# Token mixing beside a gated MLP: values and receptance projected in seven block products per projection

## What is computed

```python
x_prev = pad(x[:, :-1, :])
xk = x * time_mix_k + x_prev * (1.0 - time_mix_k)     # xv and xr alike
k = einsum('btd,ed->bte', xk, W_k)
v = einsum('btd,ed->bte', xv, W_v)
r = sigmoid(einsum('btd,ed->bte', xr, W_r))
wkv = _wkv_scan(k, v, time_decay, time_first)         # running maximum, sums weighted by exponentials
y = r * wkv
attn = einsum('btd,ed->bte', y, W_o)
...
h = silu(lin(x, w1_w, w1_s)) * lin(x, w2_w, w2_s)      # 256 -> 1024
h = gelu(lin(h, h1_w, h1_s))                           # 1024 -> 1024
h = gelu(lin(h, h2_w, h2_s))                           # 1024 -> 1024
out = lin(h, w3_w, w3_s)                               # 1024 -> 256
```

## Time and profile before

| | |
|---|---|
| median of 3 runs | 1473.9 us (1470.48 to 1475.95) |
| the profiled execution: time, span | 1469.84 us, 1468.1 us |
| TensorE busy | 1459.3 us, 99% |
| VectorE busy | 1136.9 us, 77% |
| ScalarE busy | 997.9 us, 68% |
| GpSimd busy | 99.6 us, 7% |
| granted TensorE clock | full in every slice (2.4 GHz) |
| DMA | 300.02 MB, mean 204 GB/s |

### The profile page before, as it was taken

How to read it: one execution, slowest core, us unless ns; L and a number is a source line. 1 busy time by engine, 2 the same in 40 slices (tenths; PEclk the granted TensorE clock), 3 DMA queues, 4 the chain that set the end, 5 groups by cost and what they waited for, 6 DMA issues and landing times.

```text
span 1468.1 us, 28022 instructions
## 1 busy us (share of the span) xinstructions
PE 1459.3 (99%) x10236; PEld 1314.6 (90%) x10236; DVE 1136.9 (77%) x1600; ACT 997.9 (68%) x1525; POOL 99.6 (7%) x128
## 2 busy tenths in 40 slices
PE   8999999999999999999999999999999999999999
PEld 7989898998989989898898989989899898998998
DVE  6786878778797786977868788687877869778655
ACT  7995665767657576675856757676576765757655
POOL 1112000010100101001010010100001010010100
PEclk9999999999999999999999999999999999999999
DMA  9988574755737467375674746657475674746654
GB/s 345 386 296 282 171 246 120 239 170 194 251 113 258 142 201 250 123 255 145 202 225 149 247 132 219 195 173 252 121 245 152 206 245 120 262 136 203 186 184 133
DMA packets 105374, 300.02 MB, mean 204 GB/s; under 512 B 10496, under 2 KB 41856, under 8 KB 103552
## 3 DMA queue, kind: packets, MB, share of 16 engines
q1 hardware_dynamic: 97184, 291.75, 58.4%
q0 software_dynamic: 8160, 7.87, 4.3%
HBM read 265.44 MB, written 33.09 MB: 203 GB/s over the span
## 4 chain that ended last, share of the span: by engine, by line
PE 97%; ACT 1%; DVE 1%; issue 0%; DMA 0%; POOL 0%; DVEq 0%; SPq 0%; ACTq 0%; POOLq 0%
PE acc L713 27%; PE acc L715 27%; PE att L606 11%; PE acc L687 7%; PE acc L688 7%; PE acc L739 4%; PE acc L741 4%; PE att L645 4%; PE acc L844 2%; PE acc L842 2%; PE att L585 1%; PE att L688 1%; PE att L687 1%; PE acc L813 1%; ACT early L1246 0%
## 5 line engine op out<-in xcount | busy, mean ns | idle before, releaser
L713 PE MATMUL acc<-op_hi,ring 128*128 128x256 f32 x3360 | 810.3, 286 | 0.5 <-issue 0.5
L715 PE MATMUL acc<-op_lo,ring 128*128 128x256 f32 x3360 | 788.5, 279 | 0.0
L713 PEld LDWEIGHTS acc<-op_hi,ring 128*128 128x128 f32 x3360 | 631.0, 188 | 18.6 <-issue 17.6
L715 PEld LDWEIGHTS acc<-op_lo,ring 128*128 128x128 f32 x3360 | 632.2, 188 | 11.1 <-issue 10.0
L1716 DVE TENSOR_TENSOR op_lo<-blocks,op_hi 128x1024 fp32r<-128x1024 f32 (+2 forms) x271 | 339.4, 1268 | 66.5 <-ACT op_hi L1111 60.2
L1111 ACT ACTIVATE op_hi<-blocks 128x1024 fp32r<-128x1024 f32 (+2 forms) x263 | 284.5, 1093 | 111.9 <-DVE blocks L1711 68.6
L687 PE MATMUL acc<-x_hi,w_rnd 128*128 128x512 f32 x420 | 167.1, 398 | 0.3 <-DVE blocks L1702 0.3
L688 PE MATMUL acc<-x_lo,w_rnd 128*128 128x512 f32 x420 | 166.1, 396 | 0.0
L1151 ACT ACTIVATE blocks<-acc,vec 128x256 f32<-128x256 f32 x268 | 104.9, 476 | 68.2 <-PE acc L715 60.9
L1151 ACT ACTIVATE blocks<-parts,vec 128x256 f32<-128x256 f32 x240 | 101.1, 498 | 64.1 <-DVE parts L1774 61.5
L1107 ACT ACTIVATE fresh<-acc,vec 128x512 f32<-128x512 f32 x105 | 72.1, 686 | 74.8 <-PE acc L688 74.8
(11 more groups left out here) (216 smaller groups left out, 1904.7 us busy)
## 6 DMA issues: line engine op xcount, KB each, us to landing
ring<-scratch SPq DMA_DIRECT2D x426, 512.0 KB, 4.2
scratch<-stage SPq DMA_DIRECT2D x11, 1024.0 KB, 12.2
stage<-in_w_ffn SPq DMA_DIRECT2D x10, 1024.0 KB, 10.7
x_in<-in_x SPq DMA_DIRECT2D x32, 256.0 KB, 4.6
out<-x_next SPq DMA_DIRECT2D x30, 256.0 KB, 4.4
out<-mix_v POOLq DMA_DIRECT2D x30, 256.0 KB, 4.2
mix_r<-in_x_T SPq DMA_DIRECT2D x14, 512.0 KB, 5.7
norm<-norm_rows SPq DMA_DIRECT2D x14, 512.0 KB, 4.4
```

What stands on the lines that cost most here:

```text
L713: pe.matmul(out, act(w), act(op_hi[:, k, c, :]), start=(begins and c == 0 and m % 2 == 0), stop=False, skip_group_check=True)
L715: mm = pe.matmul(out, act(w), act(op_lo[:, k, c, :]), start=False, stop=(c == QC - 1), skip_group_check=True)
```

## The change

In the loop, for values (w = 0) and receptance (w = 1), the 256x256 weight and the 256x512 input are each taken as 2x2 blocks (an input block is a chunk of channels of one sequence). The input differences T2, T3, T4 are formed beforehand: for the values by VectorE (`quad_inputs`, into `r_sb`), for the receptance by GpSimd (`receptance_inputs`, into `mix_v`). The weight sums S1 to S4 are formed once by GpSimd (`sum_mixing`), with the values' weights scaled by 0.25 first, so that their copies need no scale. Seven products of 256 columns take the place of four of 512. They stand in four parts of 2, 2, 2 and 1 products, with `att` as four quadrants: Q11, QT3, Q21, Q22. Between the parts ScalarE copies quadrants (`again`: Q11 to Q21, then Q21 to Q22 and QT3 to SBUF), VectorE adds QT3 to Q21 and Q22 (`quad_sums`), and ScalarE takes out Q11 and Q22 (`copy_quads`). The keys, tiles 0 and 1 and the output projection are as before.

```diff
@@ -144,7 +144,7 @@
-    DVE_EXTRA = 4
+    DVE_EXTRA = 2
@@ -196,6 +196,7 @@
+w_sums = overlay("w_sums", [P, 2, 4, P], F32)
@@ -285,9 +286,21 @@
+quad = [att[:, SEG * k:SEG * (k + 1)] for k in range(4)]
+Q11, QT3, Q21, Q22 = quad
+QUADS = ((mix_v, r_sb, v_sb), (mix_r, mix_v, r_sb))
+def quarters(t):
+    return t[:].rearrange("p c (n t) -> p (c n) t", n=n_seq)
...
+def by_half(ap):
+    return ap.rearrange("p (n t) -> p n t", n=n_seq)
@@ -343,7 +356,7 @@
-               Chain(ctx, nc, "dve_chain", 38), Chain(ctx, nc, "pool_chain", 2), ahead=1, seqs_ahead=0, like=FIRST[0])
+               Chain(ctx, nc, "dve_chain", 40), Chain(ctx, nc, "pool_chain", 4), ahead=1, seqs_ahead=0, like=FIRST[0])
@@ -369,6 +382,9 @@
+dve_quad, act_again, pe_part = (tally(n, k, 1, ahead=-2) for n, k in (("dve_quad", 3), ("act_again", 4), ("pe_part", 4)))
+pool_T = tally("pool_T", 1, 1, ahead=-2)
+mix_sums = ctx.enter_context(nc.semaphore("mix_sums"))
@@ -607,6 +623,36 @@
+    def product(w, bank, weights, moving, start=False, stop=False):
+        return pe.matmul(bank, weights, moving, start=start, stop=stop, skip_group_check=True)
+    def project_part(t, w, part):
+        src, sums = quarters(QUADS[w][0]), quarters(QUADS[w][1])
+        T_1, T_3, T_2, T_4 = (sums[:, k, :] for k in range(4))
+        a11, a12, a22 = (wm[:, 1 + w, c, e * P:(e + 1) * P] for e, c in ((0, 0), (0, 1), (1, 1)))
+        S_1, S_2, S_3, S_4 = (w_sums[:, w, k, :] for k in range(4))
+        if part == 0:
+            pe.wait_ge(mix_sums, 5)
+            if w == 0:
+                pe.wait_ge(dve_quad.sem, dve_quad.at(t, 1))
+            else:
+                pe.wait_ge(pool_T.sem, pool_T.at(t))
+            pe.wait_ge(WHOLE.act_kvr.sem, WHOLE.act_kvr.at(t, 2 * w + 2))
+            product(w, Q11, a11, src[:, 0, :], start=True)
+            pe_part.add(product(w, QT3, S_3, T_3, stop=True))
+        elif part == 1:
+            pe.wait_ge(act_again.sem, act_again.at(t, 2 * w + 1))
+            product(w, Q11, a12, src[:, 2, :], stop=True)
+            pe_part.add(product(w, Q21, S_2, T_2))
+        elif part == 2:
+            pe.wait_ge(WHOLE.act_kvr.sem, WHOLE.act_kvr.at(t, 2 * w + 3))
+            product(w, Q21, a22, T_4, stop=True)
+            WHOLE.pe_kvr.add(product(w, Q22, S_1, T_1))
+        else:
+            pe.wait_ge(dve_quad.sem, dve_quad.at(t, w + 2))
+            WHOLE.pe_kvr.add(product(w, Q22, S_4, src[:, 3, :], stop=True))
@@ -903,17 +949,25 @@
             step(i, 0, 0)
             step(i, 0, 1)
             pe.wait_ge(dve_prod.sem, dve_prod.at(i, 3))
-            project(WHOLE, i + 1, [0, 1, 2])
+            project(WHOLE, i + 1, [0, 1])
             step(i, 0, 2, [0])
+            project_part(i + 1, 0, 0)
             step(i, 0, 2, [1])
-            project(WHOLE, i + 1, [3])
-            step(i, 0, 3)
-            step(i, 0, 4)
+            project_part(i + 1, 0, 1)
+            step(i, 0, 3, [0])
+            project_part(i + 1, 0, 2)
+            step(i, 0, 3, [1])
+            step(i, 0, 4, [0])
+            project_part(i + 1, 0, 3)
+            step(i, 0, 4, [1])
             step(i, 0, 5)
-            project(WHOLE, i + 1, [4])
-            step(i, 0, 6)
+            project_part(i + 1, 1, 0)
+            step(i, 0, 6, [0])
+            project_part(i + 1, 1, 1)
+            step(i, 0, 6, [1])
+            project_part(i + 1, 1, 2)
             step(i, 1, 0, [0])
-            project(WHOLE, i + 1, [5])
+            project_part(i + 1, 1, 3)
             step(i, 1, 0, [1])
             step(i, 1, 1)
             step(i, 1, 2)
@@ -1047,6 +1101,20 @@
+    def again(t, w, k):
+        if k == 0:
+            act.wait_ge(pe_part.sem, pe_part.at(t, 2 * w + 1))
+            act_again.add(act.activation(Q21, Q11, ACT.Copy))
+        else:
+            act.wait_ge(pe_part.sem, pe_part.at(t, 2 * w + 2))
+            WHOLE.act_kvr.add(act.activation(Q22, Q21, ACT.Copy))
+            act_again.add(act.activation(QUADS[w][2][:, 0, 0:SEG], QT3, ACT.Copy))
+    def copy_quads(t, w):
+        act.wait_ge(WHOLE.pe_kvr.sem, WHOLE.pe_kvr.at(t, 2 * w + 4))
+        WHOLE.act_kvr.add(act.activation(by_half(QUADS[w][2][:, 0, :]), att[:].rearrange("p (k t) -> p k t", t=SEG)[:, 0::3, :], ACT.Copy))
@@ -1066,6 +1134,8 @@
         act.wait_ge(s.act_kvr.sem, s.act_kvr.at(t))
+        if not isinstance(t, int):
+            act.wait_ge(dve_quad.sem, dve_quad.at(t, 3))
         s.act_exp.add(act.activation(r_sb[:, :, s.cols], r_sb[:, :, s.cols], ACT.Tanh, scale=0.5))
@@ -1381,26 +1451,28 @@
         copy_kvr(WHOLE, i + 1, [0])
         p1(i, 0)
         copy_kvr(WHOLE, i + 1, [1])
-        copy_kvr(WHOLE, i + 1, [2])
+        again(i + 1, 0, 0)
         g11(i, 0)
+        again(i + 1, 0, 1)
         hiB11(i)
         p5(i, 0)
-        copy_kvr(WHOLE, i + 1, [3])
         hi6(i)
         u2(i, 0)
+        copy_quads(i + 1, 0)
         exp_new(WHOLE, i + 1)
         exp_old(WHOLE, i + 1)
         share(WHOLE, i + 1)
+        again(i + 1, 1, 0)
         g12(i, 0)
         g22(i, 0)
+        again(i + 1, 1, 1)
         hiB22(i)
         hiT1(i)
-        copy_kvr(WHOLE, i + 1, [4])
         g21(i, 0)
+        copy_quads(i + 1, 1)
         hiT23(i)
         p1(i, 1)
         hiB21(i)
-        copy_kvr(WHOLE, i + 1, [5])
         receptance(WHOLE, i + 1)
         p5(i, 1)
         seed_x(WHOLE, i + 1)
@@ -1545,6 +1617,24 @@
+    def quad_inputs(t):
+        b, T = quarters(QUADS[0][0]), quarters(QUADS[0][1])
+        dve.wait_ge(WHOLE.dve_mix.sem, WHOLE.dve_mix.at(t, 2 * DC))
+        link(WHOLE, dve.tensor_tensor(T[:, 0:2, :], b[:, 1::2, :], b[:, 0:2, :], ALU.subtract))
+        settle(WHOLE, t)
+        link(WHOLE, dve.tensor_tensor(T[:, 2, :], b[:, 3, :], T[:, 0, :], ALU.subtract))
+        settle(WHOLE, t)
+        dve_quad.add(dve.tensor_tensor(T[:, 3, :], b[:, 2, :], T[:, 2, :], ALU.subtract))
+    def quad_sums(t, w):
+        dve.wait_ge(WHOLE.pe_kvr.sem, WHOLE.pe_kvr.at(t, 2 * w + 3))
+        dve.wait_ge(act_again.sem, act_again.at(t, 2 * w + 2))
+        out = QUADS[w][2]
+        dve_quad.add(dve.tensor_tensor(by_half(out[:, 1, :]), by_half(att[:, 2 * SEG:]),
+                                       out[:, 0:1, 0:SEG].broadcast_to([P, 2, SEG]), ALU.add))
@@ -1598,6 +1688,8 @@
         distance(s, t)
+        if not isinstance(t, int):
+            quad_sums(t, 0)
         settle(s, t)
@@ -1610,8 +1702,10 @@
         dve.wait_ge(s.act_exp.sem, s.act_exp.at(t, 2))
-        if s is FIRST[0]:
+        if s is FIRST[0] or not isinstance(t, int):
             dve.wait_ge(s.act_kvr.sem, s.act_kvr.at(t, 2 * DC))
+        if not isinstance(t, int):
+            dve.wait_ge(dve_quad.sem, dve_quad.at(t, 2))
         new = fresh[:, :, s.cols]
@@ -1687,9 +1781,6 @@
-    def by_half(ap):
-        return ap.rearrange("p (n t) -> p n t", n=n_seq)
@@ -2013,6 +2104,7 @@
         lo23(i, 1)
+        quad_inputs(t)
         t23(i, 1)
@@ -2029,6 +2121,7 @@
         t23b(i)
+        quad_sums(t, 1)
         loT1(i)
@@ -2120,6 +2213,34 @@
+    def receptance_inputs(t):
+        b, T = quarters(QUADS[1][0]), quarters(QUADS[1][1])
+        pool.wait_ge(WHOLE.dve_mix.sem, WHOLE.dve_mix.at(t))
+        pool.wait_ge(WHOLE.pe_kvr.sem, WHOLE.pe_kvr.at(t, 4))
+        stand_alone(pool, spare, t)
+        WHOLE.pool_chain.link(pool.tensor_tensor(T[:, 0:2, :], b[:, 1::2, :], b[:, 0:2, :], ALU.subtract))
+        settle(WHOLE, t)
+        WHOLE.pool_chain.link(pool.tensor_tensor(T[:, 2, :], b[:, 3, :], T[:, 0, :], ALU.subtract))
+        settle(WHOLE, t)
+        pool_T.add(pool.tensor_tensor(T[:, 3, :], b[:, 2, :], T[:, 2, :], ALU.subtract))
+    def sum_mixing():
+        pool.wait_ge(WHOLE.pe_kvr.sem, WHOLE.pe_kvr.at(1))
+        pool.tensor_scalar(wm[:, 1, :, :], wm[:, 1, :, :], 0.25, None, ALU.mult).then_inc(mix_sums, 1)
+        pool.wait_ge(mix_sums, 1)
+        pool.wait_ge(pe_half.sem, pe_half.at(0, PLAIN_STEPS))
+        a11, a12, a21 = (wm[:, 1:3, c, e * P:(e + 1) * P] for e, c in ((0, 0), (0, 1), (1, 0)))
+        a22 = wm[:, 1:3, 1, P:2 * P]
+        s1_, s2_, s3_, s4_ = (w_sums[:, :, k, :] for k in range(4))
+        pool.tensor_tensor(s1_, a21, a22, ALU.add).then_inc(mix_sums, 1)
+        pool.tensor_tensor(s3_, a11, a21, ALU.subtract).then_inc(mix_sums, 1)
+        pool.wait_ge(mix_sums, 3)
+        pool.tensor_tensor(s2_, s1_, a11, ALU.subtract).then_inc(mix_sums, 1)
+        pool.wait_ge(mix_sums, 4)
+        pool.tensor_tensor(s4_, a12, s2_, ALU.subtract).then_inc(mix_sums, 1)
@@ -2163,8 +2284,8 @@
-    WHOLE.pool_chain.n = -1
-    pool.sem_inc(WHOLE.pool_chain.sem, WHOLE.pool_chain.per - 1)
+    WHOLE.pool_chain.n = 1
+    pool.sem_inc(WHOLE.pool_chain.sem, WHOLE.pool_chain.per + 1)
@@ -2176,9 +2297,11 @@
     next_deviation(1)
+    sum_mixing()
     add_out(0, (0, 1))
...
     with pool.Fori(1, NT - 1) as i:
+        receptance_inputs(i + 1)
         tile_deviation(i + 1, 2)
```

## The result

The changed kernel took 1528.9 us (median of 4 runs, 1528.12 to 1530.07). In the same comparison the kernel before took 1474.7 (1470.48 to 1475.95). The ratio is 1.0373, with a 95% interval of 1.0351 to 1.0396: 3.7% slower. The prediction said 1518.7, within 1496 to 1534, and slower with a chance of 0.89. The sign, the mechanism and three of its four waits were right; the time was 10 us short. The profiled execution took 1530.07 us, span 1528.4, 60.3 us more than the span before.

What follows compares the result with a forecast made beforehand. PE (TensorE), busy 99% of the span, was taken to bound the kernel. Terms of -0.83 + 2.23 + 0.78 + 0.26 + 0.76 gave +3.20 us a tile, +44.8 over 14 tiles, so 1518.7 us from 1473.9, range 1496 to 1534.

Steps and rivals of the forecast that it cites:

- four waits: PE was to wait in each tile before step 2, step 6, and parts 2 and 3 of the receptance.
- Term 1: PE's projections of values and receptance: 14 products of 256 columns replace 4 chunks, -0.83 us a tile.
- Term 2: Before step 2, PE waits for ScalarE's p1: +2.23 us a tile, 0.72 from PE's order and 1.51 from DVE.
- Term 3: Before step 6, PE waits for DVE's c22, which a shorter receptance part no longer covers: +0.78 us a tile.
- Term 4: Before part 2 of the receptance, PE waits for ScalarE's copy of Q21: +0.26 us a tile.
- Term 5: Before part 3 of the receptance, PE waits for VectorE's sums: +0.76 us a tile.
- The tile: One loop tile, 89.50 us before, was to grow by 3.20 us in sum, to 92.7 us.
- GpSimd: Its three receptance differences, priced at 1.17 and 0.6 us, were to have T4 ready 2.7 us before PE wants it.
- The first rival: GpSimd's three differences each wait for a VectorE instruction of 1.22 us: 14 us more, 1533 us; chance 7%.
- 14 tiles: +44.8: Over the whole loop, the +3.20 us a tile was counted alike in 14 tiles, giving +44.8 us.
- PE's busy share down to about 95%: Sign expected in the profile after: PE's busy share falls from 99% of the span to about 95%.
- a wait of some 2.2 us: Sign expected in the profile after: PE or its weight loads idle some 2.2 us before step 2, waiting for ScalarE's copy.

Runs made afterwards that it cites:

- Experiment 8: The kernel of experiment 6, with p1 ahead of the first key copy on ScalarE and GpSimd's weight sums behind its tile 0 DMA: 1468.1 us, ratio 0.9966.
- experiment 1: The changed kernel, with VectorE's three differences for the values moved behind lo45(i, 1), so that t23(i, 1) comes before them: 1498.9 us, ratio 1.0174.
- experiment 2: The kernel before, with only the third projection chunk (first of the values) moved behind the first half of step 2 on PE: 1485.6 us, ratio 1.0086.
- Experiment 7: The kernel of experiment 5, with VectorE's sum for the receptance moved ahead of t23b, the second layer's T2 and T3 differences: 1498.8 us, ratio 1.0174.
- Experiment 10: The kernel of experiment 5, with GpSimd's first difference made to wait for the end of VectorE's pair of roundings (loB11): 1491.9 us, ratio 1.0118.
- experiment 3: The changed kernel, with the products of the keys' second chunk done twice, as useless work in the pause before step 2: 1520.4 us, ratio 1.0317.
- experiment 9: The kernel before, with only t23(i, 1) ahead of VectorE's roundings and p1 ahead of the first key copy on ScalarE: 1473.9 us, ratio 0.9997.
- experiments 6: The changed kernel, with the receptance back in two chunks, no GpSimd differences, and t23(i, 1) ahead of VectorE's roundings: 1470.7 us, ratio 0.998.
- experiments 5: The changed kernel, with t23(i, 1) moved ahead of VectorE's roundings and the values' differences left between lo23 and lo45: 1493.8 us, ratio 1.0137.

## Why the prediction was right, and where it fell short

**Term 1 (-0.83).** Experiment 8 shows the values' half of it, -0.35 where -0.41 was expected. The receptance's half was never seen uncovered.

**Term 2 (+2.23).** PE arrived at 442.54 + 3.43 = 445.97 and started at 448.19: 2.22. Its two causes were taken apart: 1.51 for the differences (experiment 1), 0.79 for the order on PE (experiment 2; 0.72 in the prediction, 0.76 in the text ahead of that experiment).

**Term 3 (+0.78).** Part 0 of the receptance started at 466.24 in the changed kernel, so PE was free at 467.10 and step 6 started at 467.95: 0.85.

**Term 4 (+0.26).** Hardly there. Part 2 started at 472.63, on the end of the half step, and took 0.94 where a part takes 0.86: 0.08.

**Term 5 (+0.76).** Part 2 ended at 473.57 and the half step behind it at 475.44; part 3 started at 476.23: 0.79. The price came out right by two errors that cancel. By the prediction's own prices t1b starts at 630.70 + 0.38 + 1.30 + (629.82 - 628.01) = 634.19 and not at 634.08; counted from the end of part 0 (630.50 there, 467.10 here) its start at 470.79 is just that. And PE resumed 0.05 behind the end of the sums (475.50 + 0.68 = 476.18), not 0.16. Experiment 7 shows that the order of DVE's work bears on it.

**The tile.** -0.83 + 2.22 + 0.85 + 0.08 + 0.79 is 3.11. The half steps behind the first two waits took 1.95 in place of 1.87 (448.19 to 450.14, 467.95 to 469.90), which brings 3.27. Measured: 3.38; 0.11 I can't place. Predicted: 3.20.

**GpSimd.** It did not hold PE up, as the forecast had it, but it came close: T4 was ready at 465.28 (464.54 + 0.74) and PE wanted it at 466.24, 0.96 us of lead where I had worked out 2.7. The rows show why: 2.64 us for the first difference, where I took 1.17, and 0.75 and 0.74 for the others, where I took 0.6. The first rival had the right mechanism with too high a price, since only one of the three instructions met a VectorE instruction with two SBUF inputs. Experiment 10 agrees with the rule of the Trainium skill, "SBUF — State Buffer", section "SBUF: two separate sides", that the two exclude each other for a whole instruction: 2.64 us beside the pair, 1.30 behind it.

**The step that fell short** is "14 tiles: +44.8". It took every tile as alike and the clock as given. The 60.3 us of the span are: 14 x 3.38 = 47.3 for the tile; 5 x 1.62 = 8.1 for the clock, shown by experiment 3; 97.94 - 92.34 (before) - 3.38 = 2.2 more in the first loop tile; 1.6 ahead of the loop; 1.1 left over.

The 2.2 has three parts. DVE waited 3.1 us for the row of the norm in place of 0.9, and so PE waited 2.37 us for DVE in place of 0.29: +2.08. The clock fell at this pause, a sixth time: +1.62, if it cost what the others did. And PE, late by then, waited 0.50 us for p1 in place of 2.06: -1.56. Together that is 2.1.

The 1.6 is no part of the change: ahead of the loop the kernel of experiment 9 differs from before in nothing, and its loop came 1.6 later as well (117.40 against 115.79). In both the granted clock fell there, and it did not in the run before. The changed kernel, then the kernel before, in the same window:

```profile
32.00:38.00 6.00, 4.98 (x31) 4.82 (x30) 3.34 (x10) 5.92 (x14) 0.00 (x0) 0.72 0.99 401
```

```profile
32.00:38.00 6.00, 4.84 (x42) 4.68 (x41) 3.32 (x9) 5.97 (x14) 0.00 (x0) 1.00 1.01 411
```

The four profiled runs in which it fell there began their loop at 117.28 to 117.50, the eight in which it didn't at 115.79 to 116.77.

With the clock's 8.1 the forecast would have been 1526.8. I had noted "PE's busy share down to about 95%" and a wait of some 2.2 us and did not ask what such a pause does to the clock.

**What stays open.** Why five of 13 alike pauses lower the clock. The Trainium skill, "TensorE: Matmul & The Clock Gate", section "What's actually happening", says that activity is looked at in free-running windows, so that it matters how the work lies to them. That would suit five of 13; no run here shows the phase. And the wait for the norm's row in the first loop tile: 0.9 us before, 3.1 after, 1.5 and 1.7 in experiments 6 and 8, and 2.0 in experiment 9, whose kernel has no sums of weights on GpSimd; it does not follow them, and its cause was not found.

## What to carry to other kernels

Fewer products on the engine that bounds pay only where every operand is ready as much earlier: work out the lead of each operand at each seam first, and compare it with the gain (here 0.41 us a projection, against leads of under 1.2). Put the helper engine's new work behind whatever the bound engine waits for next; moving one line brought 35 of the 54 us back, and using the new form only where the seams had room brought the rest and 0.3% more. A new pause on TensorE of 2 us has a second price, its clock: filling it with useless products made this kernel faster by 8 us.

## What the runs showed of the hardware

- Pauses of 1.98 to 2.07 us in an otherwise full TensorE lowered its clock to 1.2 GHz in five of 13 tiles, from 0.95 to 1.34 us after it had resumed; pauses of 0.5 us (experiments 1 and 2) and 0.3 us (experiment 3) did so in none. Each fall cost 1.62 us. A pause of 2.34 to 2.37 us in the first loop tile lowered it in three kernels (the changed one, experiments 5 and 7) and left it full in a fourth (experiment 10).
- GpSimd's subtraction of 512 columns ran into a pair of VectorE instructions with two SBUF inputs already under way and by its times waited for both, not for one: it began 0.87 us behind the pair's start and ended 1.16 us after the second. VectorE lost nothing (2.35 us with and without it). An instruction of GpSimd can thus be put down with twice its length; released early and held, or released late, it was here ahead of PE all the same.
